# Padding rows of two experts read as one word, and a first batch's gathers given two blocks sooner

## What is computed

```python
x = x + tanh(g_xattn) * attention(layernorm(x), ctx, ctx)        # 16 heads of 8, 77 context rows
h = layernorm(x)
weights = softmax(h @ gW + gb)                                   # 15 experts
topv, topi = top_k(weights, 3)
gated = (one_hot(topi, 15) * topv[..., None]).sum(-2)
router = einsum("ebtd,bte->btd", expert_stack(h, rW1, rb1, rW2, rb2), gated)   # 128 -> 256 -> 128, gelu
x = x + tanh(g_ffn) * (shared_expert(h) + router + h)            # shared expert: 128 -> 512 -> 128
```

## Time and profile before

| | |
|---|---|
| median of three runs | 424.69 us (424.21 to 425.44) |
| the profiled execution | 424.94 us, span 422.8 us |
| PE busy | 373.8 us (88%) |
| DVE busy | 295.8 us (70%) |
| ACT busy | 275.1 us (65%) |
| POOL busy | 267.2 us (63%) |
| mean DMA rate | 157 GB/s |

### The profile page before, as it was taken

How to read it: one execution, slowest core, us unless ns; L and a number is a source line. 1 busy time by engine, 2 the same in 40 slices (tenths; PEclk the granted TensorE clock), 3 DMA queues, 4 the chain that set the end, 5 groups by cost and what they waited for, 6 DMA issues and landing times.

```text
span 422.8 us, 12465 instructions
## 1 busy us (share of the span) xinstructions
PE 373.8 (88%) x3840; PEld 333.6 (79%) x3840; DVE 295.8 (70%) x968; ACT 275.1 (65%) x609; POOL 267.2 (63%) x263
## 2 busy tenths in 40 slices
PE   3379899989999989999899988899999999999940
PEld 1257778778787878877899987799999997999930
DVE  4546767687878768776668977678767762687862
ACT  4248799889889877977666654466666666354400
POOL 8920313357868767774987987406777776777771
PEclk9859999999999999999999999999999999999985
DMA  4457865638373637744345547656666652224232
GB/s 127 128 132 203 275 156 165 193 96 232 112 210 116 190 102 233 272 140 153 118 159 175 150 139 225 220 173 187 198 196 188 194 156 82 76 76 106 76 79 63
DMA packets 57463, 66.30 MB, mean 157 GB/s; under 512 B 9300, under 2 KB 48340, under 8 KB 57400
## 3 DMA queue, kind: packets, MB, share of 16 engines
q1 hardware_dynamic: 49224, 49.17, 39.3%
q0 software_dynamic: 6800, 14.46, 11.8%
q10 hardware_dynamic: 1376, 1.88, 1.4%
HBM read 35.63 MB, written 29.29 MB: 154 GB/s over the span
## 4 chain that ended last, share of the span: by engine, by line
PE 53%; POOL 16%; issue 7%; DMA 6%; DVE 5%; ACT 5%; SPq 3%; ACTq 2%; POOLq 0%; DVEq 0%
PE psum L1464 13%; POOL k_heads L618 8%; PE psum L1325 8%; PE psum L1342 6%; PE psum L1444 4%; PE psum L1445 3%; PE psum L1446 3%; PE psum L1305 3%; PE psum L1434 3%; POOL q_stack L618 2%; ACT probs L703 2%; DMA q_stack<-q_split 2%; DVE max_cols L894 2%; DMA w_raw<-rows_by_expert 2%; POOL rstd L544 2%
## 5 line engine op out<-in xcount | busy, mean ns | idle before, releaser
L551 POOL DMA_INDIRECT rows_by_expert<-xn_all,row_of x96 | 95.3, 993 | 35.7 <-issue 19.0
L798 ACT ACTIVATE probs<-psum,b1c 128x256 f32<-128x256 f32 x152 | 63.7, 470 | 26.3 <-PE psum L1446 25.4
L1464 PE MATMUL psum<-w_all,probs 128*128 x608 | 80.1, 275 | 0.0
L1464 PEld LDWEIGHTS psum<-w_all,probs 128*128 128x128 f32 x608 | 74.2, 191 | 0.2
L703 ACT ACTIVATE probs<-psum 77x512 f32<-77x512 f32 x128 | 68.8, 587 | 5.9 <-PE psum L1325 4.5
L618 POOL DMA_INDIRECT k_heads<-outs_by_block,back_row x60 | 58.3, 972 | 22.0 <-issue 16.2
L894 DVE TENSOR_REDUCE max_cols<-psum 128x4 fp32r<-128x312 f32 x128 | 55.2, 472 | 9.5 <-PE psum L1305 9.4
L1325 PE MATMUL psum<-q_stack,k_heads 128*77 128x128 f32 x512 | 55.1, 244 | 1.5 <-ACT q_stack L695 1.4
L1325 PEld LDWEIGHTS psum<-q_stack,k_heads 128*77 128x77 f32 x512 | 43.7, 150 | 14.5 <-issue 6.1
L1032 DVE CAST w_ring<-w 128x512 fp32r x76 | 34.7, 456 | 22.1 <-issue 20.6
L1444 PE MATMUL psum<-q_parts,w_ring 128*128 128x256 f32 x152 | 49.0, 323 | 1.1 <-DVE q_parts L1020 1.1
(11 more groups left out here) (151 smaller groups left out, 777.6 us busy)
## 6 DMA issues: line engine op xcount, KB each, us to landing
w_raw<-rows_by_expert SPq DMA_DIRECT2D x76, 128.0 KB
outs_by_block<-probs SPq DMA_DIRECT2D x76, 128.0 KB
q_stack<-q_split SPq DMA_DIRECT2D x21, 256.0 KB
k_heads<-k_split SPq DMA_DIRECT2D x90, 39.0 KB
rows_by_expert<-zeros SPq DMA_DIRECT2D x27, 128.0 KB, 3.8
q_split<-q_parts SPq DMA_DIRECT2D x6, 512.0 KB
k_split<-w_all SPq DMA_DIRECT2D x8, 312.0 KB, 2.4
x_all<-in_x SPq DMA_DIRECT2D x8, 256.0 KB, 4.6
```

The lines of the kernel that those rows point to most:

```text
L551: nc.gpsimd.indirect_dma_start(xd[:, :], bass.IndirectOffsetOnAxis(ap=row_of[:, r, m:m + 1], axis=0), xn2_all[:, r * GB + m // K, :], None ...
L798: nc.scalar.activation(hid[u % 2][:, c, :], psum[:, 2 + c, 0:BLK], ACT.Gelu, bias=b1c[:, bass.ds(e * CR + (CS + c), 1)]).then_inc(gelu_don ...
L1464: ins = nc.tensor.matmul(psum[:, 4 + u % 2 * 2, b * P:(b + 1) * P], hid[u % 2][:, c, b * P:(b + 1) * P], w2_all[:, bass.ds(expert_of[u] * ...
```

## The change

Two things are edited.

1. The paddings. DVE's step 0 of the table now subtracts the experts' bases from the counts' row (into `pad_count`), waits for that by a semaphore of its own, and packs the counts of two experts into one word, odd × 4096 + even (`pad_pair`); this releases `pads_ready`. SP and ACT read a word at every even expert only and keep it in a register for the odd one; the row is worked out from the word by remainder or quotient, an addition and the multiplications for the address. In the first batch the split between t = 27 and t = 29 is now 8 and 7 experts in place of 7 and 8. POOL clears `pad_count` at the start.
2. The gathers. POOL's loop that gives the first batch's gathers begins at u = `NB` + 2 in place of `NB` + 4. With one or two a block, its blocks now hold all 48; before they held 46, and two were given after the loop.

```diff
-        pad_row = sb("pad_row", [1, 2 * E], I32)
+        pad_count = sb("pad_count", [1, EP])
+        pad_pair = sb("pad_pair", [1, EP], I32)
...
+            pad_words = {}
+
             def pad_rows(h, e):
-                row = sp.value_load(pad_row[0:1, h * E + e:h * E + e + 1], min_val=0, max_val=2 * HALF_ROWS - BLK)
-                sp.dma_start(xd[bass.ds(row, BLK), :].rearrange("(p c) d -> p (c d)", c=BC), zeros[:, 0:BC * D]).then_inc(pads_in[h], 16)
+                if e % 2 == 0:
+                    pad_words[h, e // 2] = sp.value_load(pad_pair[0:1, h * EP // 2 + e // 2:h * EP // 2 + e // 2 + 1], min_val=0, max_val=(1 << 24) - 1)
+                word = pad_words[h, e // 2]
+                count = word % AREA if e % 2 == 0 else word // AREA
+                sp.dma_start(xd[bass.ds(count + (h * HALF_ROWS + e * AREA), BLK), :].rearrange("(p c) d -> p (c d)", c=BC), zeros[:, 0:BC * D]).then_inc(pads_in[h], 16)
...
-                    for e in range(E // 2) if t == 27 else range(E // 2, E):
+                    for e in range(EP // 2) if t == 27 else range(EP // 2, E):
                         pad_rows(0, e)
...
+            pool.memset(pad_count[:], 0.0)
...
-            for u in range(NB + 4, NU):
+            for u in range(NB + 2, NU):
                 pool.wait_ge(xs_hi_ready, u + 1)
                 for n in range(given, given + (2 if u % 3 == 0 else 1)):
                     gather(n)
...
-                    nc.vector.tensor_copy(pad_row[:, h * E:(h + 1) * E], ps[0:1, 16:16 + E]).then_inc(pads_ready, 1)
+                    nc.vector.tensor_tensor(pad_count[:, 0:E], ps[0:1, 16:16 + E], expert_base[h][0:1, :], ALU.subtract).then_inc(pads_counted, 1)
+                    dve.wait_ge(pads_counted, h + 1)
+                    by_pair = pad_count[:].rearrange("a (w k) -> a w k", k=2)
+                    nc.vector.scalar_tensor_tensor(pad_pair[:, h * EP // 2:(h + 1) * EP // 2], by_pair[:, :, 1], float(AREA), by_pair[:, :, 0], ALU.mult, ALU.add
+                                                   ).then_inc(pads_ready, 1)
                     nc.vector.tensor_copy(counts[:], ps[0:EP, 0:2]).then_inc(counts_out, 1)
```

More of the change, by code:

```diff
@@ L209, in flamingo_kernel @@
         pads_ready = sem("pads_ready")
+        pads_counted = sem("pads_counted")
         zeroed = sem("zeroed")
@@ L799, in gelu @@
                                          bias=b1c[:, bass.ds(e * CR + (CS + c), 1)]).then_inc(gelu_done, 1)
+            pad_words = {}
             def pad_rows(h, e):
-                row = act.value_load(pad_row[0:1, h * E + e:h * E + e + 1], min_val=0, max_val=2 * HALF_ROWS - BLK)
-                act.dma_start(xd[bass.ds(row, BLK), :].rearrange("(p c) d -> p (c d)", c=BC), zeros[:, 0:BC * D]).then_inc(pads_in[h], 16)
+                if e % 2 == 0:
+                    pad_words[h, e // 2] = act.value_load(pad_pair[0:1, h * EP // 2 + e // 2:h * EP // 2 + e // 2 + 1], min_val=0, max_val=(1 << 24) - 1)
+                word = pad_words[h, e // 2]
+                count = word % AREA if e % 2 == 0 else word // AREA
+                act.dma_start(xd[bass.ds(count + (h * HALF_ROWS + e * AREA), BLK), :].rearrange("(p c) d -> p (c d)", c=BC), zeros[:, 0:BC * D]).then_inc(pads_in[h], 16)
             lead_rows(0)
```

## The result

The changed kernel took **422.56 us** (median of five runs, 422.21 to 423.37) against 424.69 before; the ratio is 0.9947, 95% interval 0.9931 to 0.9964. The profiled execution took 422.21 us, with a span of 420.2 against 422.8. Weighted by the widths of their intervals the three give 0.9960, so about 1.7 us less. Forecast were 2.0, and 422.7 us.

The account below looks back on a forecast made before the run. SP's in-order queue was taken to bound the expert stage from 242 to 276 us. −2.80 + 0.60 + 0.23 = −1.97 us off the profiled 424.94 gave 422.97; the median being 0.25 lower, 422.7, range 421.2 to 424.4.

Parts of the forecast that it names:

- The bound: Expert stage, 242 to 276 us: SP's in-order queue gives a block every 2.43 us or more, PE needs one every 1.79.
- The rival by which the transfers bind: SP's queue there: saved reads return as longer waits at issues, no gain, 424.7 us; chance 0.07 of no gain's 0.20.
- Fewer reads: SP's loop, second batch: five of ten padding reads go, 0.56 us each, −2.80 us.
- longer address: SP's ten second-batch paddings: more register operations per address, +0.061 us each, 0.6 us back.
- A later start: DVE's table step before SP's release: subtraction, semaphore wait and multiply-add instead of one cast, +0.23 us.
- The next limit: Second batch's first load, waiting for the last scatter to land: just fits, charged 0, up to 0.5 us.
- Covered edits: First batch's seven saved reads, behind 9 us of cover, and gathers two blocks sooner, inside POOL's wait: nothing gained.
- Issue stalls: SP's 1.57 us store issue: each new stall costs 1.25, three give 426.5 us, chance 0.07; vanishing gives 421.5.

Follow-up runs that it names:

- the three: Three comparisons of the changed kernel with the kernel before: ratios 0.9947, 0.9981 and 0.9975.
- the paddings alone: Changed kernel with the first batch's gathers begun at u = `NB` + 4 again; 423.55 us, ratio 0.9990 to the kernel before.
- gathers only: Kernel before with the first batch's gathers begun at u = `NB` + 2, paddings as before; 423.81 us, ratio 0.9981.
- first batch only: Changed kernel with packed words in the first batch only, second batch's paddings and the gathers as before; 423.64 us, ratio 0.9992 to the kernel before.
- all together: Changed kernel with SP's paddings a block later, ACT's at blocks 25 to 29, no range checks on padding and block words; 421.71 us, ratio 0.9932 to before.

## Why the prediction was right, step by step

**The bound.** SP's queue sets the blocks of this stretch. Ten reads more move SP's stretch, the stage and the time by nearly the same amounts (5.30, 4.99 and 4.76 us). From the first padding's read to the load of block 36 the queue doesn't wait: in no trace is there more than one gap between two of its instructions above 0.07 us, and that one is 0.34 to 0.37 us. The rival by which the transfers bind and a saved read comes back as a longer issue is refuted: in that stretch the 28 issues take 11.54 us in the trace before and 11.69 after (11.86 each in the mean of the three traces with unpacked and the four with packed paddings that are named below), while the stretch itself shrinks by 1.84. The Trainium skill's rule (Perfetto Trace Analysis, What "DMA-bound" means), which gave 0, doesn't describe this queue: its track is not solid with issues; before, more than half of it was register instructions and the gaps between them.

**Fewer reads, longer address (−2.80 and +0.60, so −2.20 on SP).** Four traces of packed paddings (the changed kernel three times and the paddings alone) have stretches of 23.30 to 23.59, mean 23.47; the three with unpacked ones (before, gathers only, first batch only) 25.27 to 25.96, mean 25.61: −2.14. So the sum was right in the mean, though not each of its parts. In the pair of traces that the prediction was about they came out so (rounded, from the trace's nanoseconds):

| us of SP's stretch | before | after | |
|---|---|---|---|
| reads of paddings' words | 3.17 (10) | 2.04 (5) | −1.13 |
| reads of block words | 1.09 (4) | 1.39 (4) | +0.30 |
| range checks and asserts of the paddings | 1.71 | 0.87 | −0.84 |
| addresses of the paddings | 0.44 | 0.88 | +0.44 |
| other register instructions | 2.42 | 2.32 | −0.10 |
| issues of paddings, loads, stores | 11.54 (28) | 11.69 (28) | +0.15 |
| gaps between instructions | 4.90 | 4.24 | −0.66 |
| stretch | 25.27 | 23.42 | −1.84 |

The address cost 0.044 each where 0.061 was taken. The five reads with their checks and gaps gave 2.63 where 2.80 was taken. What was not foreseen is that the reads that stay grow: 0.317 to 0.407 us for the paddings, 0.27 to 0.35 for the block words; the other two traces of the changed kernel have this too, that of the paddings alone hardly (0.31 and 0.30). That −2.14 comes so near to −2.20 is in part luck: an address taken too dear stood against reads that grew. Turns of SP from load to load, forecast as 2.5 and 1.9 to 2.0 in turn, were 2.3 to 2.6 and 1.7, with one of 4.0 around the long issue.

**A later start (+0.23).** DVE's second step starts 0.19 us after its first. SP's first read starts at 247.30 against 246.94, 0.36 later, of which 0.17 was there already at the result of block 20. So 0.19 where 0.23 was taken, and SP's wait is 4.4 as forecast.

**The next limit (charged 0, up to 0.5).** This is the term that was mis-sized, and named wrongly: not the last scatter (it starts at 269.83, within 0.2 of the forecast) but the last padding, ACT's, whose landing the first load of the second batch waits for, 0.5, 0.9 and 0.6 us in three traces of the changed kernel and 0.7 in that of the paddings alone. The trace before had shown the room: there the last padding had landed at 273.51, only 0.70 us before SP came, and it moved by no more than 0.25, to 273.26. The load went at 274.34, not at 273.15: 0.48 us of the difference is this wait, 0.15 a longer read of the block word behind it, and 0.56 that SP came there 1.41 us sooner in place of 1.97. So from −2.14 in SP's queue less comes through to the last result: the stage is shorter by 1.33 in the mean of the four traces with packed paddings, against +0.29 in the mean of the three without, a difference of 1.6. That agrees with the 1.7 of the three comparisons. The forecast of 1.97 was 0.3 too much, and the median of the first comparison, 2.13, was on the lucky side of three.

**Covered edits.** First batch: nothing that can be measured, by its own kernel. Gathers: POOL's wait grew from 2.02 to 4.45 us, 4.5 forecast; no time shown. What stays open is the 0.92 us behind the second gathers' start: their stretch was 60.1 to 60.2 us in two of the four traces with the gathers at their old place and 59.2 to 59.3 in the other two and in all nine with them moved. It may be chance or an effect of the second edit; the time of the gathers alone (0.9981, its interval holds 1) doesn't decide.

**Issue stalls.** The store's long issue neither vanished nor multiplied: 1.57 us at 261.33 before, 1.52 at 260.61 after, one in each.

```profile
260.22 0.34 SPq L417 DMA_DIRECT2D w_raw<-rows_by_expert  x1
260.61 1.52 SPq L504 DMA_DIRECT2D outs_by_block<-probs  x1
```

## What to carry to other kernels

A queue that is 3% of the chain over the whole span can set the pace of one stretch; cut the span by stages, count blocks in each, and read the queue there instruction by instruction, register instructions too. In such a queue a register read with its check costs as much as an issue and a half, so pack words and drop checks on values that are known; but ask at once which landing the first step after the stretch waits for, and list every semaphore it waits on, not only the one that looks latest. Where limits lie half a microsecond apart, move them together: here each edit alone was hard to tell from none, and all together gave 1.3 us more.

## What was unexpected in the hardware

A read of one word into a register is not of one length. In all traces the shortest is about 0.27 us, but single reads in SP's stretch took up to 0.76. In the four packed traces the second read of a padding's word, right behind SP's shortest turn (1.69 us from load to load; before, no turn was under 2.2), took 0.47 to 0.67. But a shorter turn is not needed for it: each of the four traces with ten reads of paddings' words has one long read too, of 0.50 to 0.76 us, behind a turn of 2.2 us or more. With ten reads put back the mean is 0.30 again. What lengthens a read is not shown.

The long issue near 261 us comes at the same place in most kernels whose queue differs, and it isn't tied to the store: with the gathers alone it was a load's, 1.34 us at 261.42. In the ten microseconds around it the changed kernel's queues of DMA show, besides the data, a transfer of 16 KB on a queue of the kind "instruction":

```profile
q8 instruction: 1, 0.02, 0.9%
```

This queue has 33 such transfers in the whole execution. The trace has 8490 instructions of PE, weight loads among them, which is 257 for each transfer, and 734 of SP, so these are more likely PE's instructions than SP's. The two go together in time: in the thirteen traces, between 200 and 352 us, SP has 36 issues of over 1 us, and each of them overlaps a transfer on this queue; but only half of the 155 transfers there have an issue of over 0.6 us beside them. That one causes the other wasn't tried.
